# One program for three stages; the first layer's last batch finished on the chip tile by tile

## What is computed

```python
h = layernorm(x) * (1 + ca) + sa
q, kv = (h @ Wc_down) @ Wq_up, (h @ Wc_down) @ Wkv_up
y = softmax(causal(q k^T / sqrt(8))) v                   # 16 heads, one k and v
x = x + ga * (y @ Wc_proj)
h = layernorm(x) * (1 + cb) + sb
scores = softmax(h @ Wr);  G, idx = top_k(scores.T, 1024)   # per expert, over all 4096 tokens
x = x + gb * scatter_add(idx, G * (gelu(h[idx] @ W1 + b1) @ W2 + b2))
x = x + ga2 * window_attention(layernorm(x) * (1 + ca2) + sa2)
x = x + gb2 * channel_mix(layernorm(x) * (1 + cb2) + sb2)
```

## Time and profile before

| | us |
|---|---|
| three runs: median (lowest, highest) | 1009.99 (1009.61, 1013.24) |
| the profiled execution, its own time | 1016.24 |
| its span, first to last instruction | 1014.5 |
| stage 1 up to the last value product | 0 to 441.5 |
| from there to the first routing round | 441.5 to 478.2 |
| rounds, ranks and first index list | 478.2 to 537 |
| expert stage to VectorE's last instruction | 537 to 729.7 |
| second hand-over, start of layer 2 up to its first scores | 729.7 to 778.5 |
| layer 2 | 778.5 to 1014.5 |

### The profile page before, as it was taken

The page is one execution under the profiler, slowest core; times in us unless marked ns, Lnnn a source line. Parts: engine busy times, 40 slices in busy tenths (PEclk is TensorE's granted clock), DMA queues, the critical chain, the costliest instruction groups (busy, mean ns, idle before and its releaser), DMA issues. The chain is left out here.

```text
span 1014.5 us, 16284 instructions
## 1 busy us (share of the span) xinstructions
PE 832.7 (82%) x5850; PEld 393.0 (39%) x5850; DVE 580.6 (57%) x1441; ACT 467.7 (46%) x736; POOL 433.0 (43%) x554
## 2 busy tenths in 40 slices
PE   4678898999998989952888998898646999988884
PEld 3223333343433343232433453444323555555443
DVE  3676676757686767112676333303344888878761
ACT  1004464545454545730334433333364777777651
POOL 7211020505050502234005688787475577774323
PEclk9658999889999999975999988899956999999996
DMA  5220343161413231213001233333200011010100
GB/s 127 60 58 18 90 136 87 42 176 48 95 58 82 57 85 37 63 54 88 19 0 36 41 44 43 43 44 32 31 21 22 23 23 33 22 24 22 33 11 21
DMA packets 73077, 51.92 MB, mean 51 GB/s; under 512 B 21088, under 2 KB 67176, under 8 KB 72424
## 3 DMA queue, kind: packets, MB, share of 16 engines
q1 hardware_dynamic: 63144, 43.33, 17.1%
q0 software_dynamic: 9856, 7.58, 5.7%
HBM read 32.32 MB, written 16.46 MB: 48 GB/s over the span
## 5 line engine op out<-in xcount | busy, mean ns | idle before, releaser
L639 DVE TENSOR_REDUCE MX<-bank 128x1 f32<-128x512 f32 (+3 forms) x352 | 216.2, 639 | 86.2 <-PE bank L389 81.6
L503 ACT ACTIVATE PR<-ps_s 128x1024 f32<-128x1024 f32 x160 | 158.9, 1023 | 152.9 <-PE ps_s L353 87.9
L386 PE MATMUL bank<-K,Q 96*128 96x512 bf16 (+3 forms) x512 | 136.4, 327 | 31.6 <-DVE MX L639 16.5
L386 PEld LDWEIGHTS bank<-K,Q 96*128 96x128 bf16 x512 | 44.4, 102 | 153.8 <-DVE MX L639 113.3
L344 PE MATMUL ps_s<-Q,K 99*128 99x512 bf16 x320 | 97.6, 394 | 2.0 <-DMA Q<-d_m 2.0
L1063 POOL DMA_INDIRECT d_acc<-Y,idx x56 | 87.5, 1562 | 22.3 <-issue 15.9
L389 PE MATMUL bank<-maskT,identb 128*128 128x128 bf16 (+2 forms) x352 | 92.6, 263 | 0.0
L369 PE MATMUL bank<-PR,VE 128*32 128x512 f32 x640 | 90.4, 638 | 0.2 <-ACT PR L503 0.2
L1284 PE MATMUL ps_o<-H,w 128*128 128x512 f32 x176 | 90.0, 666 | 0.0
L1272 PE MATMUL ps_h<-XT,w 128*128 128x512 f32 x176 | 88.8, 628 | 1.1 <-issue 0.5
L1053 POOL DMA_INDIRECT XG<-d_tab,idx x56 | 53.7, 959 | 81.6 <-DVE idx L1178 65.4
(11 more groups left out here) (298 smaller groups left out, 1400.2 us busy)
## 6 DMA issues: line engine op xcount, KB each, us to landing
Q<-d_q SPq DMA_DIRECT2D x24, 384.0 KB
d_q<-qs SPq DMA_DIRECT2D x24, 128.0 KB, 2.3
d_y<-ysb SPq DMA_DIRECT2D x128, 18.0 KB
d_tab<-tab SPq DMA_DIRECT2D x8, 272.0 KB, 2.4
X<-L_attn_x SPq DMA_DIRECT2D x8, 256.0 KB, 4.6
w<-L_ffn_W SPq DMA_DIRECT2D x8, 256.0 KB, 3.3
d_acc<-zrow SPq DMA_DIRECT2D x1, 2048.0 KB, 9.5
yt<-d_y SPq DMA_DIRECT2D x8, 256.0 KB, 3.4
```

The source lines that it names most:

```text
L386: nc.tensor.matmul(ps_mx[G % 2][:, x * w:(x + 1) * w], Q[b % QB][0:KR, h, P * g:P * g + P], K[b % QB][0:KR, 0:w], start=(x == 0), stop=Fal ...
L503: nc.scalar.activation(PR[t % 2][:, 2 * half:2 * half + 2, :], ps_s[half][:, :].rearrange("p (a f) -> p a f", a=2), ACT.Exp, scale=DH ** - ...
L639: nc.vector.tensor_reduce(MX[b % 2][:, c:c + len(hs)], ps_mx[G % 2][:, 0:len(hs) * w].rearrange("p (x w) -> p x w", w=w), AX_X, ALU.max).t ...
```

## The change

The three stages become functions per engine and run in one block, so that the block's barriers and branches between them go. `s_phase` stays. GpSimd's last drain of stage 2 is a memset of `mark`.

For batch 7 there is no way through DRAM. `ysb` is transposed on TensorE (`last_rows_T`), VectorE divides each row by its sum (`last_rows`), TensorE transposes back and projects, VectorE adds and normalises, GpSimd makes only the reciprocal root (`last_rstd`). Query tiles 0 to 2 go together, tile 3 follows (`TILES`). `MISC_LAST` replaces `MISC0` in n = 7. VectorE normalises batch 6 too, and copies `h2T` of batches 5 and 6. The store of the last 512 rows is waited for only by the last dense load and before the first gather.

The routing tables `biti`, `bitf`, `upper`, `upm`, `group` are made by GpSimd in n = 1, in memory that the expert stage fills later; `SCh` is written per batch. The ranks lose their copies and subtractions: `onesv` is zero at each expert's first tile, `upm` is `upper` less one, and iota is made one larger, so that `slotf` needs one operation.

In stage 3 GpSimd clears `VF`, VectorE normalises batch 0, and ScalarE issues six of the 16 key DMAs of batch 0.

```diff
-LEAD, TAIL = 2, 2
+LEAD, TAIL = 2, 1
+LB = NB - 1
+MISC_LAST = {3: [("h2", LB - 2)], 4: [("lg", LB - 2)], 6: [("pj", LB - 1)], 8: [("h2", LB - 1)], 9: [("lg", LB - 1)]}
+TILES = ((0, NT - 1), (NT - 1, NT))
...
+                if n == LB and s in (2, 4, 7):
+                    last_rows_T((2, 4, 7).index(s), ps_mx[0])
+                if n == LB and s == 8:
+                    last_outputs_T(0, ps_mx[1], 3)
+                if n == LB and s == 9:
+                    last_project(0, ps_mx[0], 4)
+                if n == NB and s == 0:
+                    last_rows_T(3, ps_misc)
+                    last_h_T(0, ps_mx[1], 6)
+                    last_outputs_T(1, ps_misc, 7)
+                    last_logits(0, ps_mx[0], 8)
+                    last_project(1, ps_misc, 9)
+                    last_h_T(1, ps_misc, 13)
+                    last_logits(1, ps_misc, 14)
...
+        def last_rows(g, bank_, done):
+
+            dve.wait_ge(tl_pe, done)
+            v4 = bank_[:, :].rearrange("p (l j x) -> p l j x", l=4, j=4)
+            r4 = qr[:, 16 * g:16 * g + 16].rearrange("p (l j) -> p l j", l=4)
+            lk(nc.vector.reciprocal(r4, v4[:, :, :, DH]))
+            nc.vector.tensor_tensor(yrows[:, g, :].rearrange("p (j l d) -> p l j d", j=4, l=4), v4[:, :, :, 0:DH],
+                                    bc(r4.unsqueeze(3), [P, 4, 4, DH]), ALU.mult).then_inc(tl_dve, 1)
...
+        def last_rstd(lo, hi):
+            lk(nc.gpsimd.tensor_scalar(ve2[:, lo:hi], mv2[:, lo:hi, 1], EPS, None, ALU.add))
+            nc.gpsimd.tensor_tensor(rs2[:, lo:hi], ve2[:, lo:hi], neghalf[:, lo:hi], ALU.pow).then_inc(tl_rs, 1)
...
-        sp.wait_ge(DS["tab_st"], 16 * NB)
+        sp.wait_ge(tl_dve, 16)
+        sp.dma_start(d_tab[T * LB:T * NB, :].rearrange("(i p) f -> p i f", p=P), tab7).then_inc(DS["tab_st"], 16)
+        sp.wait_ge(DS["tab_st"], 16 * LB)
...
-        barrier(pool, 2)
...
+        nc.gpsimd.memset(mark[:, :], 0.0).then_inc(g.s_phase, 1)
+        pool.wait_ge(g.s_phase, 10)
...
-        lk(V.tensor_copy(slotf[:, :, :], slot[:, :, :]))
-        lk(V.tensor_scalar_add(slotf[:, :, :], slotf[:, :, :], 1.0))
-        lk(V.tensor_tensor(slotf[:, :, :], slotf[:, :, :], sel[:, :, :], ALU.mult))
-        lk(V.tensor_scalar_add(slotf[:, :, :], slotf[:, :, :], -1.0))
-        lk(V.tensor_copy(stilef[:, :, :], stile[:, :, :]))
+        V.tensor_scalar(stile[:, :, :], posi[:, :, :], CAP - P, None, ALU.bitwise_and)
+        lk(V.scalar_tensor_tensor(slotf[:, :, :], slot[:, :, :], 1.0, sel[:, :, :], ALU.add, ALU.mult))
...
+                if b == 0:
+                    evacuated(act, ("kT", 0))
+                    act.wait_ge(S["kz"], 2)
+                    for h in range(NH - HACT, NH):
+                        A_.dma_start(KB[0][DH * h:DH * h + DH, h, :], KT[DH * h:DH * h + DH, :]).then_inc(k_in[0], 16)
```

More of the change, by code:

```diff
@@ L517, in _, with vector_part @@
                     nc.scalar.activation(lgx[:, :, :], lge[:, :, :], ACT.Exp).then_inc(S["lgx_rdy"], 1)
+        for (lo, hi), done in zip(TILES, (10, 15)):
+            act.wait_ge(tl_dve, done)
+            nc.scalar.activation(lgx[:, lo:hi, :], lge[:, lo:hi, :], ACT.Exp).then_inc(S["lgx_rdy"], 1)
         barrier(act, 1)
-    @block.vector
-    def _(dve):
+    def vector_part(dve):
         def lk(ins):
@@ new lines, in scaled, with shifted @@
+        def scaled(b, lo, hi):
+            for i in range(lo, hi):
+                last = nc.vector.scalar_tensor_tensor(xn2[:, i, :], X[:, NT * b + i, :], mv2[:, i, 0:1], cb[b % 2][:, 2, :],
+                                                      ALU.subtract, ALU.mult)
+            lk(last)
+        def shifted(b, lo, hi, out_):
+            for i in range(lo, hi):
+                last = nc.vector.scalar_tensor_tensor(out_[:, i, 0:D], xn2[:, i, :], rs2[:, i:i + 1], cb[b % 2][:, 1, :],
+                                                      ALU.mult, ALU.add)
+            return last
@@ L669, in _, with gpsimd_part @@
                 b = n - 2
[L670 to L679, removed]
+                if 0 <= b < LB - 2 and s == 9:
+                    gates(b, 0, NT, tab).then_inc(S["tab_rdy"], 1)
         barrier(dve, 1)
-    @block.gpsimd
-    def _(pool):
+    def gpsimd_part(pool):
         def lk(ins):
@@ L916, in program, with _ @@
     g.WT, g.GG, g.WPG, g.WVG, g.BPG, g.m1, g.gmean = WT, GG, WPG, WVG, BPG, m1, gmean
-    moe(nc, ctx, g)
+    stages = [(tensor_part, scalar_part, vector_part, gpsimd_part, sync_part), moe(nc, ctx, g)]
     mid.close()
-    block1(nc, ctx, g, out)
+    stages.append(block1(nc, ctx, g, out))
+    block = ctx.enter_context(nc.Block())
+    @block.tensor
+    def _(pe):
+        for stage in stages:
+            stage[0](pe)
+    @block.scalar
+    def _(act):
+        for stage in stages:
+            stage[1](act)
+    @block.vector
+    def _(dve):
+        for stage in stages:
+            stage[2](dve)
+    @block.gpsimd
+    def _(pool):
+        for stage in stages:
+            stage[3](pool)
+    @block.sync
+    def _(sp):
+        for stage in stages:
+            stage[4](sp)
 def moe(nc, ctx, g):
@@ L1698, in _, with scalar_part @@
                     values(U - 1)
-    @block.scalar
-    def _(act):
+    def scalar_part(act):
         A_ = nc.scalar
@@ L1838, in _ @@
                 U = NU * n + u
+                if n == -LEAD1 and u == 0:
+                    dve.wait_ge(acc_in, 16)
+                    lk(V.tensor_tensor(AC[:, :, :], AC[:, :, :], bc(GG[:, 0:1, :], [P, NT, D]), ALU.mult))
+                    V.tensor_tensor(X[:, 0:NT, :], X[:, 0:NT, :], AC[:, :, :], ALU.add).then_inc(S["xadd"], 1)
+                if n == -LEAD1 and u == 3:
+                    dve.wait_ge(S["rs"], 1)
+                    for i in range(NT):
+                        last = V.tensor_scalar(xn[:, i, :], X[:, i, :], mv[:, i, 0:1], rs[:, i:i + 1], ALU.subtract, ALU.mult)
+                    last.then_inc(S["xn"], 1)
                 b = n + 1
```

424 lines of the change are left out of this document (269 added, 155 removed).

## The result

The changed kernel takes 997.93 us in the median of 4 runs (995.35 to 1001.22), beside 1009.8 us (1006.01 to 1013.24) for the kernel before: a ratio of 0.987, 95% interval 0.9838 to 0.9903. It is faster, as forecast, but by 11.9 us and not by 24.8, and 997.9 us lies above the end of the forecast range, 994.5. The profiled execution took 997.41 us, with a span of 995.3.

What follows compares the result with a forecast made beforehand. TensorE was taken as the bound or close to it inside the stages; the change targets the gaps between them. Terms -19.0 + 2.2 - 3.5 - 2.6 - 1.9 = -24.8 us gave a 985.2 us median, range 978.5 to 994.5.

Steps and rivals of the forecast that it cites:

- Part 1: End of layer 1: TensorE's added work moves the last value product to 445.4, VectorE's chain ends at 457.3 us.
- Rival (b): End of layer 1: last tiles run in series, chain ends at 464.3, not 457.3; time 992.2 us; chance 0.12.
- Part 2: Hand-over to routing: first count 19.0 us earlier, late dense rows cost 2.2 us (0 if early, 4 if store delays).
- Part 3: Routing after the rounds: fewer VectorE operations shorten TensorE's waits for sel and R, -3.5 us (limit 4.0).
- Part 4: Second hand-over, after the experts: memset instead of GpSimd's 7.08 us drain, -2.6 us; 0.45 if held as long.
- rival (a): Second hand-over: GpSimd's memset is held like its drain, 2.1 us not gained, time 987.3 us; chance 0.10.
- Part 5: Start of layer 2: key loads split over two queues bring scores 4.0 us sooner, net -1.9 us; bounds 0 and -4.
- Rival (d): Start of layer 2: splitting the key loads gives nothing, time 987.1 us; chance 0.05.
- The base of the sum: Whole program: 24.8 us off the profiled 1016.24 gives 991.4, then 6.25 off for the median gives 985.2 us.
- Late signals: Expert stage: three times VectorE starts 5.0 us on average after TensorE's lists are done, 15.0 us in all.
- rival (c): Expert stage: VectorE's three late starts after TensorE's lists go away, time 979.9 us; chance 0.08.
- (e): Experts' seven index lists: each delayed signal costs 5.1 us, making the kernel slower, 1015.6 us; chance 0.03.

Runs made afterwards that it cites:

- the early load: Changed kernel, drain behind memset, first dense rows loaded before the last table store: 998.29 us; also with all key loads on SyncE: 994.09, 988.48 us.
- the pair above: Changed kernel with a drain behind the memset, on one chip: with six key loads on ScalarE 993.86 us, with all on SyncE 994.07 us.

## Why the prediction was wrong

**Part 1, the end of layer 1: right.** TensorE's added work: 3.9 us forecast. The last product started at 446.3, 440.5 and 442.1 after, 440.9 and 441.4 before, so the spread hides it in these. All kept traces together show it: 438.5 on average in the five with the old tail (436.0 to 441.4), 442.1 in the thirteen with the new one (438.5 to 446.3), which is 3.6 later. At a granted clock of 0.93 over this stretch it is 436.0 and 436.4 against 439.6 and 440.5. Both profiled executions of the kernel before had a clock of 0.91 there. The tail is 0.7 us longer than worked out: VectorE's last gate copy comes 12.6 us after the last product's end, not 11.9, and its waits are 1.34 us (forecast 0.7), 0.69 (0.5) and 0.27 (0.3). Rival (b), tiles in series, is out: no wait is over 1.5 us.

**Part 2, the hand-over: right in the barrier, short in the rows.** Start to first count: -20.0 against -19.0. For the dense rows I took 4.8 us after the issue and +2.2; the upper bound, 4, was for a store in flight that holds up the load. The trace shows that in part. The first load takes 0.67 us to issue and the second 2.04, 2.75 together; in the kernel with the old tail, whose store has landed, they take 0.58 each. The first rows are there after 5.5 us, in place of 4.2 to 4.4. But the second issue goes on until 1.3 us after the store has landed (461.99), and with no store in flight the third and fourth loads take up to 1.7 us as well. So the store's share and that of the loads ahead in the queue are not told apart. The stretch is 3.3 us longer. In it the granted clock was 0.85, against 0.90 before; with the early load it was 0.91.

**Part 3, the routing chain: right.** -3.1 against -3.5, alike in every execution with the change (the forecast's own terms, 1.4 + 2.6 - 0.4, add up to 3.6, and to 3.4 if R's wait of 2.4 us bounds the second); TensorE's waits for sel and R are gone from the list of waits in 503 to 523.

**Part 4, the memset: the step that failed.** "A memset replaces this drain. I take it at the price of a memset." The row was 7.08 us without a visible reason, and rival (a) asked only whether the memset would be held as well. It isn't. But the drain's 7 us did not go with it: the next drain on GpSimd took them, here the closing one, +4.6 us, where nothing runs beside it. The closing drain lasts 8.41 us if GpSimd has not drained since its last scatters, and 1.37 if it has. The 3.9 us that a drain in a better place gave back in the time would have put the measured 997.9 at 994.0, just inside the range. Besides, the 2.6 us that it was to save were a feature of one execution: in the second one 0.6 us lay between VectorE's end (730.83) and the next stage (731.47).

```profile
728.62 2.21 DVE L1194 SCALAR_TENSOR_TENSOR X<-ps_o,gate,X 128x128 f32<-128x128 f32 x8 [6.62 <-PE ps_o L1301]
...
731.47 7.03 ACT L1704 ACTIVATE KB<-zrow 128x8192 f32<-128x8192 f32 x1 [2.51 <-PEq L1460]
```

In the first, GpSimd's drain began 4.8 us ahead of VectorE's end, here 7.8. Forecast -2.6, measured about -0.1 + 4.6.

**Part 5, the start of layer 2: mis-sized.** The scores came 4.0 us sooner, as worked out, and QKN of batch 1 only 1.2 to 2.4 sooner, counted from the fill (1.3 worked out). What I took from it, that the stage would keep 1.9 us, had no step behind it, and it is wrong: QKN waits in VectorE's ordered queue and holds what stands behind it. The loop gave back 2.6 us, in the pair above 3.9 (199.8 and 203.8), and with the split 0.3 us more lie outside the span (2.1 and 1.8). Rival (d) was right. The Trainium skill (DMA: Bandwidth & Descriptors, Issuing engines are not separate DMA queues) says that starting DMAs from several engines saves only the sequencer's time, usually small beside the DMA. The time agrees that there is little to gain (0.997 and 1.000); the reason here is another, since the issue did cost 10.8 us and was saved in part.

**The base of the sum.** The forecast took 24.8 us off an execution of 1016.24 and then the same 6.25 off for the median. The terms that failed come to 8.7 us (24.8 - 16.1): 4.6 for the end, 2.5 in the expert stretch, 1.1 in the rounds, 0.5 in the loop, 0.4 in the routing, 0.6 elsewhere, less 1.0 gained. The other 4.2 (16.1 - 11.9) are the base: a difference between long executions of one kernel and ordinary ones of the other is not the difference of medians. Part of it can be seen: in both profiled executions of before the first layer ran at the low clock of 0.91, and its last product started at 440.9 and 441.4, against 436.0 to 437.9 in the other three traces with the old tail, whose clock there was 0.92 to 0.93.

**Late signals, rivals (c) and (e).** They were in the profiles of all eight kernels of two chips and in none of the eight of two others, whatever the program; the version with the memset, a drain behind it and no split has none on one chip and 14.6 us of VectorE's waits on another. So they go with the chip and not with the change. That they went away between the two first profiles (rival (c)) gained nothing that can be seen, as the run of the kernel before without them shows. Their price depends on where they fall. On one chip, in the three kernels that stem from the changed one, the first late signal falls ahead of the first expert's rows, and ScalarE and then TensorE wait, here in the version with the memset and a drain behind it:

```profile
522.50 0.17 DVE L1379 COPY lst<-ps_l 128x16 f32<-128x16 f32 x1 [5.40 <-remote]
526.78 0.78 ACT L1628 ACTIVATE YD<-ps_o,b2g,gbT 128x512 f32<-128x512 f32 x1 [10.32 <-remote]
```

From the first gather to the first product Y it then takes 42.5 to 43.5 us in place of 32.3 to 34.0; in the kernel before on the same chip, with the memset, 34.1. On the other chip the late signals cost this stretch nothing (33.2 to 34.0). So (e) names a mechanism that the change is open to, of some 9 us on one chip of four, where the versions with the tail are still 1.2 to 1.6% faster. What makes the signals late stays open.

## What to carry to other kernels

A drain that is taken away is not paid until the next drain on that engine has been found: follow the cost forward to the end of the program, and put the drain where its engine is idle and others work. Here one line behind the memset brought back 3.9 us (0.996, 0.9925 to 0.999). A step that moves work between engines is priced where the moved work's reader stands in its own queue, not where the transfer ends. And a gap read from one execution should be seen in a second before it is put into a sum.

## What the runs showed of the hardware

GpSimd's drain after indirect transfers that had been waited for took 7.08 to 7.23 us after 112 of them, 6.60 after 80, 2.80 after 32, and 0.03 to 1.37 where none had been issued since (0.43 at line 295 before, 0.69 at line 312 after and 1.37 at the end of the program, both beside an operation of GpSimd that was still running). With a 512-row table store in flight the first dense rows landed 5.4 to 5.6 us after their issue, instead of 4.2 to 4.4. With the changed kernel's six DMAs on ScalarE's queue 2.0 to 2.15 us lay outside the span in every execution, without them 1.7 to 1.9, but for one execution of 2.2; in the version with the old tail and the split only four executions of ten had the longer time (2.19 to 2.34).
